# Three lag matrices loaded instead of made, the down weights turned last, the clip sigmoids earlier

## The chip, the cores and the metric

The kernel runs on one core of a Trainium2 chip. Its time is device microseconds (us) of one launch; lower is better. The engines of the core are named as in the profile: PE (TensorE) for matrix products, PEld for its weight loads, DVE (VectorE), ACT (ScalarE), POOL (GpSimd), and SP (SyncE), which here issues nearly all DMAs. Each engine works through its own list of instructions in the order of the code, and semaphores tie the lists together.

## The reference

The layer adds two gated branches to x (32 sequences of 128 tokens, 256 channels). The first is a two-sided decaying sum over time of the context (keys and values are both `ctx`), times the sigmoid of the normalised x. The second is a gated feed-forward network on fake-quantised activations and weights.

```python
def birwkv(r, k, v, w, u):                 # w, u: one value a channel
    ew, ek = exp(w), exp(k)
    Af, Bf = scan(ek, v, ew)               # A_t = sum_{i<t} e^{(t-1-i)w + k_i} v_i;  B_t without v
    Ab, Bb = the same from the other end
    cur = exp(u + k)
    return sigmoid(r) * (Af + Ab + cur * v) / (Bf + Bb + cur)

def quant(x, clip):                        # one scale for the whole tensor
    s = sigmoid(clip) * max|x| / 127
    return clip(round(x / s), -128, 127) * s

x = x + tanh(g_xattn) * birwkv(layernorm(x), ctx, ctx, w, u)
z = quant(layernorm(x), clip_x)
h = quant(silu(z @ Wg.T) * (z @ Wu.T), clip_down)
x = x + tanh(g_ffn) * (h @ Wd.T)           # each W quantised with a scale for each row
```

## The kernel before

**Stages.** The whole of x stays in SBUF. (1) x and ctx are loaded; ctx is turned round in time by PE (`reverse`), and exp(k) and exp(k)·v are kept in `hidden`. (2) The sum over time is, for each channel, a product with a 128x128 matrix of decays ("lag matrix"). The 256 channels are worked in 32 chunks of 8 channels; `accumulate(j)` is chunk j: eight matrices, each times 64 or 128 columns. (3) Second layernorm, `turn_z` (transposes on PE) and the largest value. (4) Quantisation, gate and up products, the largest value again. (5) Quantisation, down products, the last addition and the stores.

**Lag matrices.** The 8 matrices of a chunk are 512 KB. They lie in a ring of six slots of `hidden`. For 26 chunks SP loads them by one DMA each from a small table in HBM, `lag_dram`, whose rows are read with an overlapping pattern (`load_lags`, L265). For the six chunks of `MADE` (10, 14, 18, 22, 26, 30) they are computed instead: ACT takes eight exponentials (`make_lags`, L591, L598), POOL multiplies the flipped identity by exp(u)-1 (`own_weights`, L375, L382, two halves) and adds it (`add_own`, L387, L392, two halves). A slot comes free for chunk j when chunk j-6 has been used (`ab_done`). PE waits for the DMA (`ring_in`) or for POOL (`made`).

**A chunk's way.** After `accumulate(j)` DVE computes the denominator into `den`, which lies in h_space (`denominator`, L735); for each pair m of chunks ACT takes Ln and Exp of it (`reciprocal`, L505 and L508); DVE multiplies (`mix`, L747), and POOL adds the pair to x (`residual`, L399). DVE's list takes denominators and mixes by turns: den(2m+2), mix(2m), den(2m+3), mix(2m+1). The last pair goes by halves (L516, L519, L407, and `residual_own` at L757 on DVE). A chunk's bank in PSUM, one of six, comes free when the chunk six before has been mixed (`mix_done`).

**Other work between the chunks.** The three weight matrices are loaded, and for each DVE finds the scales of its rows (`weight_scales`, L686 to L688), ACT quantises (L542) and casts it (L550), PE turns it (`turn_weights`, L969, behind chunks 14, 23 and 30) and ACT keeps it (L559). For the third, the down weights, DVE also scales two 128x128 identities (`down_diagonals`, L775). These stand in DVE's list behind pair 9. From pair 10 on DVE takes six layernorm statistics a pair of the half of x that is already final (`early_stats`, L704). The sigmoids of the two clip values are an Exp on ACT (`exp_clips`, L564, L566, at pair 12) and four small instructions on DVE (`sigmoid_clips`, L769, L770, at pair 13).

**Behind the chunks.** `late_stats` on DVE, four tiny powers and products on POOL (`rstd2`, L367 to L373), the normalisation on ACT (L527) and POOL (L433), `turn_z` on PE (L981) and `keep_z` on ACT (L534). Between groups 3 and 6 PE runs five products whose result isn't used (`idle_wide`, L1004).

Of the kernel before, what the change touches and what calls it, by code (L numbers as in the profile page):

```python
# [40 lines left out]
def gated_rwkv_ffn(nc, x, ctx_kv, g_xattn, g_ffn, w, u, clip_x, clip_down, w_gate, w_up, w_down, out):  # L41
# [19 lines left out]
    LAGS = 2 * T - 1  # L61
    SLOTS = 6

    MADE = 10, 14, 18, 22, 26, 30
    BANKS = 6
    HALF = CK * SEQS

# [3 lines left out]
    with ExitStack() as stack:  # L71
# [39 lines left out]
        def loads_to(n):  # L111

            return len([i for i in range(n % SLOTS, n + 1, SLOTS) if i - GROUPS not in MADE])

        def lag_tile(j):
            return ring[(GROUPS + j) % SLOTS].rearrange("p (g t) -> p g t", t=T)
# [133 lines left out]
        def _(sp):  # L250
# [14 lines left out]
            def load_lags(j):  # L265

                before = GROUPS + j - SLOTS
                if before < GROUPS:
                    sp.wait_ge(s["ctx_back"], before + 1)
                else:  # L270
                    sp.wait_ge(s["ab_done"], before - GROUPS + 1)
                src = bass.AP(lag_dram, j * CK * LAGS, [[1, P], [LAGS, CK], [1, T]])
                sp.dma_start(lag_tile(j), src).then_inc(ring_in[(GROUPS + j) % SLOTS], 16)  # L273
# [36 lines left out]
            for j in range(CHUNKS):  # L310
                if j not in MADE:
                    load_lags(j)
# [20 lines left out]
        def _(pool):  # L333
# [41 lines left out]
            def own_weights(i):  # L375

                j = MADE[i]
                pool.wait_ge(s["u_all_done"], 2)
# [8 lines left out]
            def add_own(i):  # L387
                for h in range(2):
                    pool.wait_ge(s["made_exp"], 2 * i + h + 1)
                    pool.wait_ge(s["own_done"], 2 * i + h + 1)  # L390
                    part = lag_tile(MADE[i])[:, h * CK // 2:(h + 1) * CK // 2, :]
                    nc.gpsimd.tensor_tensor(part, part, own_parts[h].rearrange("p (g t) -> p g t", t=T),  # L392
                                            ALU.add).then_inc(s["made"], 1)
# [25 lines left out]
            for m in range(PAIRS - 1):  # L419
                residual(m)  # L420
                j = 2 * (m + 1) + 6
                if j in MADE:
                    add_own(MADE.index(j))
                    if j != MADE[-1]:
# [44 lines left out]
        def _(act):  # L469
# [31 lines left out]
            def reciprocal(m):  # L501

                act.wait_ge(s["den_done"], 2 * m + 2)
                wait(act, s["rden_done"], m)
                nc.scalar.activation(lnd, den[:, m % 2, :], ACT.Ln).then_inc(s["ln_done"], 1)  # L505
                act.wait_ge(s["ln_done"], m + 1)
                wait(act, s["mix_done"], 2 * m - 2)
                nc.scalar.activation(rden[:, m % 2, :], lnd, ACT.Exp, scale=-1.0).then_inc(s["rden_done"], 1)  # L508
# [28 lines left out]
            def quantise_weights(m):  # L537

                act.wait_ge(s["w_rec"], m + 1)
                cols, parts, inverse = (C, KA, w_inv[:, m, :]) if m < 2 else (KA * P, CH, down_inv)  # L540
                for i in range(parts):
                    last = nc.scalar.activation(w_int[:, i * cols:(i + 1) * cols], w_nat[m][:, i * cols:(i + 1) * cols],  # L542
                                                ACT.Copy, scale=inverse[:, i:i + 1])
                last.then_inc(s["w_quant"], 1)

            def cast_weights(m):

                act.wait_ge(s["w_quant"], m + 1)
                wait(act, s["w_turned"], m)
                nc.scalar.activation(w_intb[:, :], w_int[:, :], ACT.Copy).then_inc(s["w_cast"], 1)  # L550

            def keep_weights(m):

                act.wait_ge(s["w_turned"], m + 1)
                banks = ps[:, TURN:TURN + 2, 0:KA * P // 2].bitcast(BF16)
                dst = (wgT[:, :, :], wuT[:, :, :], wdT[:, :, :].rearrange("p k (h n) -> p h k n", n=P))[m]
                if m == 2:
                    banks = banks.rearrange("p h (k n) -> p h k n", n=P)
                nc.scalar.activation(dst, banks, ACT.Copy).then_inc(s["w_stored"], 1)  # L559

            def exp_clips():

                act.wait_ge(s["clx_in"], 16)
                nc.scalar.activation(S["sgx"], S["clx"], ACT.Exp, scale=-1.0).then_inc(s["clips_done"], 1)  # L564
                act.wait_ge(s["cld_in"], 16)
                nc.scalar.activation(S["sgd"], S["cld"], ACT.Exp, scale=-1.0).then_inc(s["clips_done"], 1)  # L566
# [24 lines left out]
            def make_lags(i):  # L591

                j = MADE[i]
                act.wait_ge(s["lag_abs_done"], 1)
                act.wait_ge(s["ab_done"], j - SLOTS + 1)
                for c in range(CK):
                    n = j * CK + c
                    last = nc.scalar.activation(lag_tile(j)[:, c, :], lag_abs, ACT.Exp, scale=w_all[:, n:n + 1])  # L598
                    if c % (CK // 2) == CK // 2 - 1:
                        last.then_inc(s["made_exp"], 1)  # L600

            for m in range(PAIRS - 1):
                reciprocal(m)
                if 2 * m + 6 in MADE:
                    make_lags(MADE.index(2 * m + 6))
                if m in (3, 7, 11):
                    quantise_weights((3, 7, 11).index(m))
                if m in (9, 13):
                    keep_weights((9, 13).index(m))
                if m in (5, 9, 13):  # L610
                    cast_weights((5, 9, 13).index(m))
                if m == 12:
                    exp_clips()
            for j in (CHUNKS - 2, CHUNKS - 1):
                reciprocal_half(j)
# [50 lines left out]
        def _(dve):  # L666
# [60 lines left out]
            def denominator(j):  # L727

                dve.wait_ge(s["ab_done"], j + 1)
                if j == 0:  # L730
                    dve.wait_ge(s["ez_done"], GROUPS)
                m, i = j // 2, j % 2
                if i == 0:
                    wait(dve, s["ln_done"], m - 1)
                nc.vector.scalar_tensor_tensor(den[:, m % 2, i * HALF:(i + 1) * HALF].rearrange("p (c b) -> p c b", b=SEQS),  # L735
                                               ez[:, :, j * CK:(j + 1) * CK].rearrange("p b c -> p c b"), 1.0, half_bank(j, 0),
                                               ALU.add, ALU.mult).then_inc(s["den_done"], 1)

            def mix(j):
                m, i = j // 2, j % 2  # L740
                if m < PAIRS - 1:
                    dve.wait_ge(s["rden_done"], m + 1)
                else:
                    dve.wait_ge(s["rden_half"], i + 1)
                if i == 0:
                    wait(dve, s["x1_done"], m - 1)
                nc.vector.scalar_tensor_tensor(mixed[:, m % 2, i * CK:(i + 1) * CK, :], half_bank(j, 1), S["tanh_x"],  # L747
                                               rden[:, m % 2, i * HALF:(i + 1) * HALF].rearrange("p (c b) -> p c b", b=SEQS),
                                               ALU.mult, ALU.mult).then_inc(s["mix_done"], 1)
# [45 lines left out]
            for m in range(PAIRS - 2):  # L795
                denominator(2 * m + 2)
                mix(2 * m)
                denominator(2 * m + 3)
                mix(2 * m + 1)
                if m == 2:  # L800
                    weight_scales(0)
                if m == 6:
                    weight_scales(1)
                if m == 9:
                    weight_scales(2)
                    dve.wait_ge(s["ident_set"], 2)
                    down_diagonals()
                if m == 13:
                    sigmoid_clips()
                if m > 9:  # L810
                    early_stats(done, 6)
                    done += 6
# [120 lines left out]
        def _(pe):  # L933
# [27 lines left out]
            def turn_weights(m):  # L961

                pe.wait_ge(s["w_cast"], m + 1)
                wait(pe, s["w_stored"], m)
                for h in range(CH):
                    bank = ps[:, TURN + h, 0:KA * P // 2].bitcast(BF16)
                    for k in range(KA):
                        at_ = k * C + h * P if m < 2 else (h * KA + k) * P
                        last = nc.tensor.transpose(bank[:, k * P:(k + 1) * P], w_intb[:, at_:at_ + P], ident_b[:, :])  # L969
                last.then_inc(s["w_turned"], 1)  # L970
# [25 lines left out]
                    idle_products(5)  # L996
            for j in range(CHUNKS):
                accumulate(j)
                if j in (14, 23, 30):
                    turn_weights((14, 23, 30).index(j))  # L1000
            def idle_wide(n):

                for i in range(n):
# [110 lines left out]
```

## Time and profile before

| | us |
|---|---|
| three runs, median (lowest to highest) | 217.41 (217.23 to 217.84) |
| the profiled execution, its own time | 216.45 |
| its span, first to last instruction | 214.6 |
| busy: PE, DVE, ACT, POOL | 171.4, 171.0, 156.1, 137.6 |
| moved by DMA | 29.30 MB |

Time outside the span is 1.85 us. The profiled execution lies 0.96 us below the median of the runs. The chain of work that ended last names PE for 35% of the span, DVE for 22%, ACT for 15% and DMA for 9%. The chunks run from about 37 to 100 us, the second layernorm from there to 126 us.

### The profile page before, as it was taken

How to read it: one execution, taken by the hardware profiler on the slowest of the kernel's cores; microseconds unless marked ns; L12 is line 12 of the kernel's file. 1: busy time of each engine (PE TensorE's matmuls, PEld its weight loads, DVE VectorE, ACT ScalarE, POOL GpSimd, SP SyncE). 2: the span in 40 equal slices, each digit the busy share in tenths (PEclk: the TensorE clock that was granted, in tenths of full speed). 3: DMA queues.
4: the chain of work that ended last, by engine and by line, in shares of the span. 5: the costliest groups of instructions: out<-in, count | busy, mean ns of one | idle time of the engine just before them, and what ended most of it. 6: DMA issues, size and time to landing. Idle time of an engine off the chain costs nothing.

```text
span 214.6 us, 3377 instructions
## 1 busy us (share of the span) xinstructions
PE 171.4 (80%) x1121; PEld 124.1 (58%) x1126; DVE 171.0 (80%) x346; ACT 156.1 (73%) x237; POOL 137.6 (64%) x158
## 2 busy tenths in 40 slices
PE   4499977979899999974079888599799925989950
PEld 4456527979899999974057543234243403766620
DVE  0769495546657779999789779997999998999992
ACT  3459698555887896997789978588789834899300
POOL 3364223458599889995788808759886750039991
PEclk9969997999999999999556999999999995799995
DMA  3999999999999997300000000000000000004558
GB/s 92 346 358 348 349 322 292 286 283 292 290 305 292 227 260 220 101 2 2 0 0 0 0 5 0 0 0 0 3 0 0 0 0 0 3 0 147 175 195 268
DMA packets 43327, 29.30 MB, mean 137 GB/s; under 512 B 2224, under 2 KB 43056, under 8 KB 43312
## 3 DMA queue, kind: packets, MB, share of 16 engines
q1 hardware_dynamic: 43168, 28.84, 47.0%
q10 hardware_dynamic: 144, 0.26, 0.3%
q8 instruction: 9, 0.15, 0.3%
q14 instruction: 6, 0.05, 0.1%
HBM read 24.65 MB, written 4.46 MB: 136 GB/s over the span
## 4 chain that ended last, share of the span: by engine, by line
PE 35%; DVE 22%; ACT 15%; DMA 9%; issue 7%; SPq 6%; POOL 3%; DVEq 1%; ACTq 0%
PE ps L1050 9%; PE ps L1083 9%; PE ps L941 7%; PE ps L957 7%; DMA hidden<-lag_w 6%; DVE hidden L847 4%; DMA hidden<-in_ctx 3%; ACT hidden L527 3%; SPq L273 2%; DVE h_space L904 2%; DVE hidden L865 2%; PE ps L988 2%; DVE h_peaks L876 2%; ACT hidden L598 2%; ACT silu_out L648 2%
## 5 line engine op out<-in xcount | busy, mean ns | idle before, releaser
L957 PE MATMUL ps<-hidden 128*128 128x128 f32 (+1 forms) x512 | 60.6, 280 | 5.7 <-DVE hidden L678 2.5
L957 PEld LDWEIGHTS ps<-hidden 128*128 128x128 f32 x512 | 59.5, 196 | 7.2 <-DMA hidden<-lag_w 5.7
L876 DVE TENSOR_REDUCE h_peaks<-hidden (+2 forms) x24 | 25.9, 1122 | 2.0 <-POOL hidden L452 1.3
L1083 PE MATMUL ps<-wdT,z_t 128*128 128x256 bf16 (+1 forms) x192 | 25.2, 286 | 2.7 <-ACT z_t L662 2.7
L735 DVE SCALAR_TENSOR_TENSOR h_space<-z_t,ps 128x256 f32<-128x256 f32 x32 | 19.0, 597 | 10.2 <-PE ps L957 10.0
L399 POOL TENSOR_TENSOR x_all<-x_all,silu_out 128x512 f32<-128x512 f32 x15 | 22.8, 1533 | 6.1 <-DVE silu_out L747 6.0
L662 ACT ACTIVATE z_t<-h_space 128x1024 bf16<-128x1024 int8 (+3 forms) x12 | 20.1, 1754 | 6.8 <-DVE h_space L904 6.8
L1083 PEld LDWEIGHTS ps<-wdT,z_t 128*128 128x128 bf16 (+1 forms) x192 | 17.1, 101 | 10.8 <-issue 4.8
L648 ACT ACTIVATE silu_out<-ps,mix_scale 128x1024 f32<-128x1024 f32 (+1 forms) x18 | 18.4, 1020 | 5.8 <-PE ps L1050 3.4
L465 POOL TENSOR_TENSOR x_all<-x_all,z_t 128x512 f32<-128x512 f32 x6 | 10.7, 1803 | 15.5 <-DVE z_t L922 15.5
L981 PE MATMUL ps<-ident,hidden 128*128 128x128 f32 x64 | 11.8, 345 | 10.4 <-POOL hidden L433 9.0
L497 ACT ACTIVATE z_t<-x_all,mr,nr 128x256 f32<-128x256 f32 x32 | 16.4, 589 | 3.7 <-POOL mr L361 3.7
L941 PE MATMUL ps<-hidden,flip 128*128 128x512 f32 x32 | 16.1, 645 | 3.2 <-DMA hidden<-in_ctx 3.2
L747 DVE SCALAR_TENSOR_TENSOR silu_out<-ps,small,silu_out 128x256 f32<-128x256 f32 x32 | 15.2, 477 | 4.3 <-ACT silu_out L508 2.6
L452 POOL TENSOR_TENSOR hidden<-silu_out,up_out 128x1024 f32<-128x1024 f32 x6 | 14.4, 2408 | 5.6 <-ACT up_out L652 5.4
L696 DVE BATCH_NORM_STATS2 bn<-x_all 128x6 f32<-128x256 f32 x32 | 11.2, 413 | 8.0 <-DMA x_all<-in_x 7.8
L452 POOL TENSOR_TENSOR hidden<-h_space 128x1024 f32<-128x1024 f32 x6 | 14.4, 2400 | 4.8 <-ACT h_space L652 4.8
L981 PEld LDWEIGHTS ps<-ident,hidden 128*128 128x128 f32 x64 | 9.7, 181 | 13.1 <-ACT hidden L527 11.8
L505 ACT ACTIVATE up_out<-h_space 128x512 f32<-128x512 f32 x15 | 9.3, 623 | 9.3 <-DVE h_space L735 9.3
L904 DVE TENSOR_SCALAR h_space<-hidden,small 128x1024 int8<-128x1024 f32 (+3 forms) x12 | 15.2, 1332 | 0.1
L356 POOL TENSOR_TENSOR ve<-mv,consts 128x4 f32<-128x4 f32 x8 | 1.6, 200 | 20.4 <-DVE mv L700 20.4
L598 ACT ACTIVATE hidden<-down_row,xq 128x128 f32<-128x128 f32 x48 | 14.6, 388 | 0.0
(109 smaller groups left out, 357.3 us busy)
## 6 DMA issues: line engine op xcount, KB each, us to landing
hidden<-lag_w SPq DMA_DIRECT2D x26, 512.0 KB, 7.3
x_all<-in_x SPq DMA_DIRECT2D x8, 512.0 KB, 8.8
hidden<-in_ctx SPq DMA_DIRECT2D x8, 512.0 KB, 9.1
out<-x_all SPq DMA_DIRECT2D x16, 256.0 KB, 2.4
xq<-in_L_ffn_w_down SPq DMA_DIRECT2D x1, 704.0 KB, 6.1
xq<-in_L_ffn_w_gate SPq DMA_DIRECT2D x1, 640.0 KB, 7.0
h_space<-in_L_ffn_w_up SPq DMA_DIRECT2D x1, 640.0 KB, 5.9
lag_w<-up_out ACTq DMA_DIRECT2D x1, 255.0 KB, 7.4
```

The lines of the kernel that those rows point to most:

```text
L399: nc.gpsimd.tensor_tensor(xs, xs, mixed[:, m % 2, :, :].rearrange("p c b -> p b c"), ALU.add).then_inc(s["x1_done"], 1)
L452: nc.gpsimd.tensor_tensor(hidden[:, b * HB + k * BT:b * HB + (k + 1) * BT], silu_even[n % 2], up_even[n % 2], ALU.mult).then_inc(s["h_even ...
L648: nc.scalar.activation(silu_out[:, 1, 0:cols] if k % 2 else silu_even[even % 2], banks[0], ACT.Silu, scale=mix_scale[:, 0, k:k + 1]).then_ ...
L662: nc.scalar.activation(hq[:, b % 2, cols], h8[:, b % 2, cols], ACT.Copy).then_inc(s["hq_done"], 1)
L735: nc.vector.scalar_tensor_tensor(den[:, m % 2, i * HALF:(i + 1) * HALF].rearrange("p (c b) -> p c b", b=SEQS), ez[:, :, j * CK:(j + 1) * C ...
L876: nc.vector.tensor_reduce(h_peaks[:, bass.ds(KA * b + k, 1)], hidden[:, bass.ds(b * HB + k * BT, cols)], AX.X, ALU.max, apply_absolute_val ...
L904: nc.vector.tensor_scalar(h8[:, b % 2, k * BT:last], hidden[:, b * HB + k * BT:b * HB + last], S["inv_h"], None, ALU.mult).then_inc(s["h8_ ...
L941: last = nc.tensor.matmul(turned(g)[:, half], flip[:, :], ring[g % SLOTS][:, half], start=True, stop=True)
L957: last = nc.tensor.matmul(ps[:, j % BANKS, c * 2 * SEQS:end * 2 * SEQS], lag_tile(j)[:, c, :], ekp[:, (j * CK + c) * 2 * SEQS:(j * CK + en ...
L981: last = nc.tensor.transpose(ps[:, z_bank(g) + h, i * T:(i + 1) * T], z_all[:, n * C + h * P:n * C + (h + 1) * P], ident[:, :])
L1050: last = nc.tensor.matmul(dst, wT[:, h, k * P:k * P + rows_], whole_x(b)[:, j, h, :], start=(h == 0), stop=(h == CH - 1))
L1083: last = nc.tensor.matmul(ps[:, 4 * sl + i, j * C:(j + 1) * C], lhs, rhs, start=(k == 0 and j == 0), stop=(k == KA - 1), skip_group_check= ...
```

## The change

Chunks 22, 26 and 30 leave `MADE`: SP loads their matrices like the others', ACT no longer takes their exponentials, and POOL no longer builds and adds for them. The turning of the down weights moves from between chunks 30 and 31 to behind chunk 31. The Exp of the clips moves from pair 12 to pair 9 on ACT, the rest of their sigmoids from pair 13 to pair 10 on DVE.

```diff
-    MADE = 10, 14, 18, 22, 26, 30
+    MADE = 10, 14, 18
...
-                if m == 12:
+                if m == 9:
                     exp_clips()
...
-                if m == 13:
+                if m == 10:
                     sigmoid_clips()
...
             for j in range(CHUNKS):
                 accumulate(j)
-                if j in (14, 23, 30):
-                    turn_weights((14, 23, 30).index(j))
+                if j in (14, 23):
+                    turn_weights((14, 23).index(j))
+            turn_weights(2)
+
             def idle_wide(n):
```

POOL's list, from the additions for chunk 22 (L392) to the first half residual (L407). `up_out` and `own` are the two halves of the products of `own_weights`; L399 is a residual. Before:

```order
L392 TENSOR_TENSOR hidden<-hidden,up_out 128x512
L392 TENSOR_TENSOR hidden<-hidden,own 128x512
L382 TENSOR_TENSOR up_out<-flip,xq 128x512
L382 TENSOR_TENSOR own<-flip,xq 128x512
L399 TENSOR_TENSOR x_all<-x_all,silu_out 128x32x16 x2
L392 TENSOR_TENSOR hidden<-hidden,up_out 128x512
L392 TENSOR_TENSOR hidden<-hidden,own 128x512
```

After, all that is left between the additions for chunk 18 and the end of the stage:

```order
L392 TENSOR_TENSOR hidden<-hidden,up_out 128x512
L392 TENSOR_TENSOR hidden<-hidden,own 128x512
L399 TENSOR_TENSOR x_all<-x_all,silu_out 128x32x16 x9
L407 TENSOR_TENSOR x_all<-x_all,silu_out 128x32x8
L407 TENSOR_TENSOR x_all<-x_all,silu_out 128x24x8
```

So twelve instructions of L382 and L392 are gone there, and nine residuals follow each other directly.

PE's list, from chunk 30 to the first transpose of the next stage (L981), with the semaphores waited for, as one piece of the difference:

```order
-L957 MATMUL ps<-hidden 128x128 [waits mix_done,made]
+L957 MATMUL ps<-hidden 128x128 [waits mix_done,ring_in2]
+L957 MATMUL ps<-hidden 128x128 x6
+L957 MATMUL ps<-hidden 128x64
+L957 MATMUL ps<-hidden 128x128 [waits mix_done,ring_in3]
 L957 MATMUL ps<-hidden 128x128 x6
 L957 MATMUL ps<-hidden 128x64
 L969 MATMUL ps<-ident_b,w_intb 128x128 [waits w_stored,w_cast]
 L969 MATMUL ps<-ident_b,w_intb 128x128 x11
-L957 MATMUL ps<-hidden 128x128 [waits mix_done,ring_in3]
```

Chunk 30 now waits for a DMA, not for POOL, and the wait for ACT's cast (`w_cast`) stands behind chunk 31.

## Rows read from the trace of the kernel before

**Rows 1.** The page, 40 slices of 5.4 us: PE's granted clock in tenths.
```profile
PEclk9969997999999999999556999999999995799995
```

**Rows 2.** Windows of 10 us: busy us of each engine, clock, DMA share, GB/s.
```profile
70.00:80.00 10.00, 9.73 (x88) 9.59 (x87) 7.06 (x15) 9.22 (x20) 8.62 (x8) 1.00 0.96 242
80.00:90.00 10.00, 10.00 (x98) 10.00 (x97) 9.86 (x22) 7.83 (x17) 9.71 (x9) 1.00 0.65 187
```

**Rows 3.** Timeline of DVE at pair 9: start, us, instruction, [idle before, releaser].
```profile
77.95 0.48 DVE L747 SCALAR_TENSOR_TENSOR silu_out<-ps,small,silu_out 128x256 f32<-128x256 f32 x1 [1.16 <-ACT silu_out L508]
...
79.26 1.74 DVE L686 TENSOR_REDUCE small<-xq 128x2 f32<-128x1536 f32 x1
81.04 0.83 DVE L687 TENSOR_SCALAR small<-small 128x2 f32<-128x2 f32 x1
...
81.98 2.65 DVE L775 TENSOR_SCALAR down_diag<-ident,small 128x128 f32<-128x128 f32 x2
```

**Rows 4.** Timeline of POOL over the same time.
```profile
80.30 3.03 POOL L399 TENSOR_TENSOR x_all<-x_all,silu_out 128x512 f32<-128x512 f32 x2
83.28 1.28 POOL L392 TENSOR_TENSOR hidden<-hidden,up_out 128x512 f32<-128x512 f32 x1
```

**Rows 5.** Timeline of DVE: the same scaling for the two other weight matrices.
```profile
53.75 0.17 DVE L687 TENSOR_SCALAR w_scale<-w_scale 128x6 f32<-128x6 f32 x1
...
69.60 0.86 DVE L687 TENSOR_SCALAR w_scale<-w_scale 128x6 f32<-128x6 f32 x1
```

**Rows 6.** Groups of DVE by form: count, busy us, mean ns of one.
```profile
L852 DVE TENSOR_SCALAR hidden<-z_t,small 128x512 int8<-128x512 f32 x2 | 0.9, 484 | 0.2 <-DVE small L839 0.2
```

**Rows 7.** Timeline of PE, chunks 22 to 31 (16 records a chunk) and the turns.
```profile
78.21 3.79 PE L957 MATMUL ps<-hidden 128*128 128x128 f32 x32 [0.27 <-POOL hidden L392]
...
82.50 10.88 PE L957 MATMUL ps<-hidden 128*128 128x128 f32 x96
94.27 2.00 PE L957 MATMUL ps<-hidden 128*128 128x128 f32 x16 [0.89 <-POOL hidden L392]
96.93 0.84 PE L969 MATMUL ps<-ident_b,w_intb 128*128 128x128 bf16 x12 [0.66 <-ACT w_intb L550]
97.61 1.95 PE L957 MATMUL ps<-hidden 128*128 128x128 f32 x16
```

**Rows 8.** Timeline of DVE over the last pairs.
```profile
94.60 0.60 DVE L735 SCALAR_TENSOR_TENSOR h_space<-z_t,ps 128x256 f32<-128x256 f32 x1
...
95.50 0.15 DVE L769 TENSOR_SCALAR small<-small 128x1 f32<-128x1 f32 x1
...
96.27 1.26 DVE L704 BATCH_NORM_STATS2 bn<-x_all 128x6 f32<-128x128 f32 x6
97.44 0.59 DVE L735 SCALAR_TENSOR_TENSOR h_space<-z_t,ps 128x256 f32<-128x256 f32 x1
...
99.60 0.58 DVE L735 SCALAR_TENSOR_TENSOR h_space<-z_t,ps 128x256 f32<-128x256 f32 x1
...
101.63 0.27 DVE L757 TENSOR_TENSOR x_all<-x_all,silu_out 128x64 f32<-128x64 f32 x1
```

**Rows 9.** Timeline of ACT: the eight exponentials for chunk 22.
```profile
74.31 2.43 ACT L598 ACTIVATE hidden<-down_row,xq 128x128 f32<-128x128 f32 x8
```

**Rows 10.** SP: the last eight loads (timeline); issue to landing from 64 us on.
```profile
69.55 17.08 SPq L273 DMA_DIRECT2D hidden<-lag_w  x8
...
DMA to landing us min/median/max: 3.9/4.5/7.7
```

**Rows 11.** Timeline of PE in the stage behind the chunks.
```profile
112.76 1.94 PE L981 MATMUL ps<-ident,hidden 128*128 128x128 f32 x8 [0.79 <-POOL hidden L433]
...
116.81 1.03 PE L1004 MATMUL ps<-wgT,ident_b 128*128 128x512 bf16 x4
...
120.07 1.06 PE L981 MATMUL ps<-ident,hidden 128*128 128x128 f32 x8 [0.20 <-issue]
```

**Rows 12.** Window of 2 us, as rows 2; clock before the DMA's two figures.
```profile
116.00:118.00 2.00, 1.95 (x12) 1.28 (x12) 1.75 (x10) 2.00 (x4) 1.76 (x6) 0.90 0.00 0
```

## The prediction, made before the changed kernel was timed

> **What bounds the kernel now.** I read windows of 10 us first, then the timeline of each engine around what the diff touches, and last the slices for the clock. In the window from 80 to 90 us PE and DVE are both full, 10.00 and 9.86 us of 10 [rows 2]. With two engines at the limit, the question is whose lag is carried to the last chunk. PE takes 10.88 / 6 = 1.81 us a chunk when it waits for nothing [rows 7], so 3.62 us a pair. DVE's work of a pair is shorter: a denominator and its mix take 95.50 - 94.60 = 0.90 us, the six statistics 97.44 - 96.27 = 1.17, so a pair 2 x 0.90 + 1.17 = 2.97 [rows 8]. DVE would therefore wait for PE, but it doesn't, since at pair 9 it fell behind: it is busy with the down weights' scales from 79.26 to 84.63, while chunks 22 and 23 were long done, at 78.21 + 3.79 = 82.00 [rows 3, 7]. It catches up 0.6 us a pair and meets PE again only at chunk 31, whose denominator at 99.60 stands right behind the product's end, 97.61 + 1.95 = 99.56 [rows 7, 8]. PE for its part lost time to POOL before chunks 22 and 30 (0.27 and 0.89 us) and to the cast and the turn before chunk 31 [rows 7].
>
> **DVE's long block is a wait in disguise.** The scaling L687 of two elements takes 0.83 us at pair 9, and 0.86 us at the second matrix, but 0.17 us at the first [rows 3, 5]. At pair 9 it starts at 81.04 inside POOL's first residual (80.30 + 1.51 = 81.81) and ends at 81.87. The first diagonal starts at 81.98 inside the second residual, which ends at 83.33; the second follows, beside POOL's addition from 83.28 to 84.56, and ends at 84.63 [rows 3, 4]. Each of the three ends 0.06 to 0.1 us after a POOL instruction: they stand still until POOL's is over. The sigmoids' scaling of one element took 0.15 us with POOL busy, so not every scaling is held [rows 8].
>
> **Part 1, the three chunks loaded.**
> ACT loses three times eight exponentials, 2.43 us each time [rows 9]. At pair 8 this lets ACT start the Ln of pair 9 1.2 us sooner (it needs a denominator that is there), so DVE no longer stands 1.16 us before mix 18 [rows 3]. But denominator 21 behind it has to wait for chunk 21, which ends at 77.94, just before PE's wait [rows 7]; so the block of the down weights starts only 0.4 us sooner, at 78.9.
> POOL loses for each of the chunks two additions of 1.28 us [rows 4] and two products. What follows at pair 9 changes: residual 9 needs mix 19, and runs from about 79.0 to 80.55; residual 10 needs mix 21, which comes after the block. The reduce takes 1.74 us to 80.6 (I assume it isn't held: it took that beside POOL before), then L687 finds POOL idle. I take its 0.17 us [rows 5], and 0.25 us for a diagonal of 128 elements, between 0.17 for six and 0.48 for 512 [rows 5, 6]. The block then ends at about 78.9 + 1.78 + 0.2 + 0.2 + 0.5 = 81.6 instead of 84.63: 3.0 us sooner. From there the next pair needs chunk 23, done at 81.6 too.
> PE starts chunk 22 at 77.9 instead of 78.21, turns the up weights, whose cast is ready, and runs chunks 24 to 31 without a break: 82.50 - 0.3 + 8 x 1.81 = 96.7 instead of 99.56. DVE now waits for PE by chunk 29: that ends at 82.2 + 6 x 1.81 = 93.1, so denominator 29 comes at 93.1 instead of 94.60, 1.5 us sooner.
> SP and the DMAs: three more loads, 1.57 MB, in a stretch where the DMA engines moved 242 and 187 GB/s [rows 2]. The ring lets load j go when chunk j-6 is used. A load took 4.5 us to land [rows 10]; at 0.96 busy the engines moved 242 GB/s, so 0.524 MB costs between 1.81 us (if 290 GB/s are had) and 2.1 us (by 242 / 0.96 = 252). No row shows eleven in a stretch here; I take 1.8, as PE and loads kept step before. Chunk 21's was issued at 69.55 (the first of the last eight) [rows 10] and lands at about 74.0; ten more at 1.81 put chunk 31's at 92.1, at 2.1 us at 95.0; PE wants it at 94.9. So the loads hide, at the bad end just. Nothing else is queued behind them on SP until the stores.
> One thing goes the other way. At 69.60 the second matrix's L687 stood beside a product of POOL, which is gone; residual 6 takes its place and lasts 1.51 us [rows 4, 5], so L687 may end up to 0.65 us later. DVE's 1.16 us of idle time at mix 18 [rows 3] takes that in.
>
> **Part 2, the sigmoids.** They move from pair 13, 95.50 to 96.27 (0.77 us) [rows 8], to pair 10. There they sit in DVE's catching up, before it waits for PE, and cost nothing; in the tail they were all on the path: 0.77 us gained. Had the block not shrunk, DVE would be bound in both places and the move would be worth 0. ACT's Exp of the clips at pair 9 takes 0.2 us where ACT has time.
>
> **Part 3, the turn.** Chunk 31 no longer stands behind the cast (0.66 us) and the turn (0.67 us, 96.93 to 97.61) [rows 7]. This is in the 96.7 above. Left where it was, the turn would put chunk 31's end at 97.4 while DVE reaches that denominator at about 97.2: worth 0.2 us. In its new place ACT keeps the turned weights only after the last pair's Exp; the turn is done by 97.6, so nobody waits.
>
> **The sum.** Denominator 29 comes 1.5 us sooner, and from it to `residual_own` at 101.63 [rows 8] the tail is shorter by 0.77 (sigmoids) and about 0.1 (small waits for ACT and PE): 2.4 us. `residual_own` at 99.2 starts the statistics, and all behind is a chain through POOL, ACT and PE that moves as one. For the profiled execution: 216.45 - 2.4 = 214.05. It lay 0.96 below the median of the runs; for the median I predict 217.41 - 2.4 = **215.0 us**, by itself between 214.4 and 215.7, the spread of 0.6 of the runs included.
>
> By the Trainium skill (SBUF — State Buffer, Who interferes with whom) a `tensor_scalar` in a two-port mode and a GpSimd instruction lock each other out wholly for the length of the first, and whoever issues first wins. By that rule the hold is gone once POOL has nothing at that moment, and the kernel comes to the 215.0 above; if the block were simply 5.4 us long, to some 216.4. The trace speaks for the rule: 0.83 against 0.17 us for the same instruction [rows 3, 5].
>
> **Rivals.**
> *The hold stays* (0.13). Residual 9 starts when mix 19 ends and lasts 1.51 us, the reduce 1.74 us: L687 finds POOL idle by only 0.1 us. One residual under a diagonal holds the block 1.3 us, as before. DVE then is bound to the end: 0.4 sooner, plus about 0.6, so 217.41 - 1.0 = 216.4.
> *The loads end last* (0.06). If a load costs 2.1 us the gain is 2.0; at 2.3 us chunk 31 ends about where it did before, so 217.3, and above that the kernel is slower. Against: the engines are at 0.65 from 80 us on [rows 2].
> *Slower by the clock* (0.05). PE's clock is at its lower level, 1.2 GHz, after the chunks (fives and a six) [rows 1], and is back at 2.4 GHz from about 116.4: 0.90 of a 2 us window [rows 12]. PE now falls idle 2.4 us sooner too, so I let the return move along. If it doesn't, a group with idle products costs at the lower level 1.94 + 5 x 2 x 0.26 = 4.5 us against a pitch of (120.07 - 112.76) / 3 = 2.44 [rows 11]: 2.1 us a group. From a bit more than one such group on the change loses; two give 217.41 - 2.4 + 4.2 = 219.2. For it: the return need not follow the work, and I can't tell from one trace what holds it. Against: before, it came while PE ran nothing but transposes, ahead of the first idle product at 116.81 [rows 11, 12], and the transposes move along.
> The Trainium skill (TensorE: Matmul & The Clock Gate, Part 4: PE-mode transpose) says transposes don't count as busy for the clock gate. By it the clock returns only behind the idle products, which is this rival. The trace disagrees: it came back at 116.4 before the first of them.
> *More* (0.06). An earlier return of the clock gives up to 0.9 us (the first transposes, 1.94 against 1.06) [rows 11]: about 214.3.
>
> **The numbers.** Forecast 0.70; hold 0.13, loads 0.06, clock 0.05, more 0.06. The range 214.1 to 216.6 takes in forecast, hold and more, less their tails: about 0.85. A measurement can tell 0.3%, 0.65 us. Faster than that: 0.70 + 0.11 + 0.06 = 0.87; within it 0.06 (weak hold, half of the loads); slower 0.07.
>
> **What would show it.** Right: L775 twice under 0.6 us together, first denominator of pair 10 at 81.7; no wait of PE for a DMA after chunk 22; chunks 24 to 31 in 14.5 us; `residual_own` at 99.2; the clock back by 116.4. Wrong: L775 over 1 us; PE waiting for `ring_in`; a second group of idle products at 1.2 GHz.

## The result: 213.8 us in the first measurement, 2.4 to 2.6 us gained over many executions

| | before | after |
|---|---|---|
| first measurement, median (lowest to highest) | 217.32 us (216.35 to 217.84), 4 | 213.82 us (213.55 to 214.46), 4 |
| ratio | | 0.985, interval 0.981 to 0.989 |
| the profiled execution | 216.45 us | 214.46 us |
| its span | 214.6 us | 212.7 us |
| busy PE, DVE, ACT, POOL | 171.4, 171.0, 156.1, 137.6 | 170.4, 168.3, 149.3, 124.5 |
| moved by DMA | 29.30 MB | 30.88 MB |
| all executions of the study, mean (lowest to highest) | 217.34 us (214.84 to 220.26), 93 | 214.73 us (213.03 to 216.40), 18 |

I had predicted 215.0 us, between 214.1 and 216.6. The change is faster, as forecast, but the measured 213.82 lies below the range. The last line of the table came out of the experiments and turns out to be what matters: the gain is 2.6 us with a standard error of 0.23 (from 0.97 / sqrt(93) and 0.91 / sqrt(18)), not 3.5. Twelve of the 93 executions before count as slow, being over 1.5% above the fastest of their measurement; the ratios in this document leave such executions out, and without them the mean before is 217.14 us and the gain 2.4 us.

The trace of the changed kernel shows the steps nearly to the letter. DVE at pair 9, timeline (compare [rows 3]):

```profile
79.52 1.75 DVE L686 TENSOR_REDUCE small<-xq 128x2 f32<-128x1536 f32 x1
81.30 0.17 DVE L687 TENSOR_SCALAR small<-small 128x2 f32<-128x2 f32 x1
81.50 0.17 DVE L688 RECIPROCAL small<-small 128x2 f32<-128x2 f32 x1
81.59 0.59 DVE L775 TENSOR_SCALAR down_diag<-ident,small 128x128 f32<-128x128 f32 x2
82.21 0.60 DVE L735 SCALAR_TENSOR_TENSOR h_space<-z_t,ps 128x256 f32<-128x256 f32 x1
```

POOL at that time, after (compare [rows 4]):

```profile
79.69 1.54 POOL L399 TENSOR_TENSOR x_all<-x_all,silu_out 128x512 f32<-128x512 f32 x1 [2.02 <-DVE silu_out L747]
84.17 1.54 POOL L399 TENSOR_TENSOR x_all<-x_all,silu_out 128x512 f32<-128x512 f32 x1 [2.94 <-DVE silu_out L747]
```

The residual ends at 79.69 + 1.54 = 81.23 and L687 starts at 81.30, 0.07 us later. L687 takes 0.17 instead of 0.83 us, the diagonals 0.59 together instead of 2.65, and the block from L686 to the last diagonal 2.66 us instead of 5.37. PE, after (compare [rows 7]):

```profile
64.75 3.74 PE L957 MATMUL ps<-hidden 128*128 128x128 f32 x32
69.43 12.72 PE L957 MATMUL ps<-hidden 128*128 128x128 f32 x112 [0.95 <-DMA hidden<-lag_w]
81.99 0.83 PE L969 MATMUL ps<-ident_b,w_intb 128*128 128x128 bf16 x12
82.66 14.46 PE L957 MATMUL ps<-hidden 128*128 128x128 f32 x128
96.95 0.83 PE L969 MATMUL ps<-ident_b,w_intb 128*128 128x128 bf16 x12
```

Chunks 24 to 31 are one stretch of 14.46 us (128 records), with no wait for POOL, a load or ACT's cast. The one wait, 0.95 us at 69.43, is for chunk 17's load, ahead of everything that the change touches. DVE over the last pairs, after (compare [rows 8]):

```profile
93.58 0.60 DVE L735 SCALAR_TENSOR_TENSOR h_space<-z_t,ps 128x256 f32<-128x256 f32 x1 [0.52 <-PE ps L957]
94.10 0.47 DVE L747 SCALAR_TENSOR_TENSOR silu_out<-ps,small,silu_out 128x256 f32<-128x256 f32 x1
94.49 1.25 DVE L704 BATCH_NORM_STATS2 bn<-x_all 128x6 f32<-128x128 f32 x6
...
97.57 0.58 DVE L735 SCALAR_TENSOR_TENSOR h_space<-z_t,ps 128x256 f32<-128x256 f32 x1
...
99.60 0.27 DVE L757 TENSOR_TENSOR x_all<-x_all,silu_out 128x64 f32<-128x64 f32 x1
```

DVE waits for PE at denominator 29, and the statistics follow mix 27 without the sigmoids between. `residual_own` comes at 99.60 instead of 101.63, 2.03 us sooner, and that is the 1.99 us by which the profiled executions differ. The clock after, on the page (compare [rows 1]):

```profile
PEclk9969999999999999999557999999999995899995
```

The clock comes back to 2.4 GHz at 114.6 us, from a granted clock of 0.86 in the window from 114 to 116, against 116.4 before: 1.8 us sooner, with the work.

So the two traces say 2.0 us, my sum 2.4, the first medians 3.5. The experiments had to settle two questions: is the mechanism the one I gave, and where do the other 1.5 us come from.

### The profile page after: what moved, and what is told of

The parts are those of the page before. It is cut to its first block, busy times and chain, and to the rows that moved or that the text cites. A ratio compares the mean times of both kernels' runs of the same rounds, so it can differ in the third digit from the quotient of the medians.

```text
span 212.7 us, 3337 instructions
## 1 busy us (share of the span) xinstructions
PE 170.4 (80%) x1126; PEld 123.2 (58%) x1126; DVE 168.3 (79%) x346; ACT 149.3 (70%) x213; POOL 124.5 (59%) x146
## 2 busy tenths in 40 slices
DMA packets 46448, 30.88 MB, mean 145 GB/s; under 512 B 2272, under 2 KB 46176, under 8 KB 46432
## 4 chain that ended last, share of the span: by engine, by line
PE 45%; DVE 21%; DMA 10%; ACT 10%; issue 5%; SPq 3%; POOL 3%; DVEq 1%; ACTq 0%
PE ps L957 19%; PE ps L1052 9%; PE ps L1085 9%; DMA hidden<-lag_w 7%; PE ps L941 5%; DVE hidden L847 4%; DMA hidden<-in_ctx 4%; ACT hidden L527 3%; PE ps L988 2%; DVE h_space L904 2%; DVE hidden L865 2%; DVE h_peaks L876 2%; ACT silu_out L648 2%; DVE bn L704 2%; ACT z_t L534 2%
## 5 line engine op out<-in xcount | busy, mean ns | idle before, releaser
L957 PE MATMUL ps<-hidden 128*128 128x128 f32 (+1 forms) x512 | 58.5, 276 | 6.1 <-DMA hidden<-lag_w 3.7
L957 PEld LDWEIGHTS ps<-hidden 128*128 128x128 f32 x512 | 57.8, 192 | 7.4 <-DMA hidden<-lag_w 7.3
L399 POOL TENSOR_TENSOR x_all<-x_all,silu_out 128x512 f32<-128x512 f32 x15 | 23.1, 1541 | 19.2 <-DVE silu_out L747 19.2
L735 DVE SCALAR_TENSOR_TENSOR h_space<-z_t,ps 128x256 f32<-128x256 f32 x32 | 19.0, 598 | 10.4 <-PE ps L957 10.1
L981 PE MATMUL ps<-ident,hidden 128*128 128x128 f32 x64 | 11.8, 346 | 10.2 <-POOL hidden L433 8.7
L696 DVE BATCH_NORM_STATS2 bn<-x_all 128x6 f32<-128x256 f32 x32 | 11.2, 414 | 8.6 <-DMA x_all<-in_x 8.3
L981 PEld LDWEIGHTS ps<-ident,hidden 128*128 128x128 f32 x64 | 9.8, 182 | 12.9 <-ACT hidden L527 11.6
L1052 PE MATMUL ps<-xq,wuT 128*128 128x512 bf16 (+1 forms) x48 | 11.5, 381 | 3.6 <-DVE hidden L865 3.5
L988 PEld LDWEIGHTS ps<-ident,flip 128*128 128x128 f32 x64 | 11.1, 261 | 5.3 <-POOL ident_b L345 2.8
```

Source lines behind the costliest of these rows:

```text
L399: nc.gpsimd.tensor_tensor(xs, xs, mixed[:, m % 2, :, :].rearrange("p c b -> p b c"), ALU.add).then_inc(s["x1_done"], 1)
L957: last = nc.tensor.matmul(ps[:, j % BANKS, c * 2 * SEQS:end * 2 * SEQS], lag_tile(j)[:, c, :], ekp[:, (j * CK + c) * 2 * SEQS:(j * CK + en ...
L981: last = nc.tensor.transpose(ps[:, z_bank(g) + h, i * T:(i + 1) * T], z_all[:, n * C + h * P:n * C + (h + 1) * P], ident[:, :])
L1052: last = nc.tensor.matmul(dst, wT[:, h, k * P:k * P + rows_], whole_x(b)[:, j, h, :], start=(h == 0), stop=(h == CH - 1))
```

## The experiments

Each had its expectation on record before it ran. Since the executions of one kernel turned out to spread over 3 to 5 us, I read small differences not from the medians but from distances inside a trace: from DVE's denominator 20 (start of its L735) to `residual_own`, which is the stretch that the change touches; from `residual_own` to the first gate product; and from there to the largest value of h (L834).

| kernel | median us (executions) | ratio to before, interval | den. 20 to residual_own | to first gate product | to the peak of h |
|---|---|---|---|---|---|
| before, first trace | 217.32 (4) | | 25.44 | 26.80 | 49.06 |
| r1_before | 217.19 (12) | 0.9986, 0.9955 to 1.0016 | 25.07 | 27.12 | 50.39 |
| after, first trace | 213.82 (4) | 0.9848, 0.9807 to 0.9889 | 22.77 | 26.83 | 49.06 |
| r1_after | 214.80 (6) | 0.9861, 0.9803 to 0.9918 | 22.78 | 26.89 | 50.58 |
| r3_after | 215.27 (8) | 0.9910, 0.9871 to 0.9948 | 22.76 | 26.82 | 49.05 |
| r1_chunks | 216.17 (12) | 0.9934, 0.9890 to 0.9977 | 23.55 | 27.47 | 50.38 |
| r1_moves | 217.84 (12) | 1.0017, 0.9980 to 1.0053 | 25.61 | 26.80 | 50.65 |
| r2_hold | 216.83 (10) | 0.9980, 0.9936 to 1.0024 | 24.15 | 26.78 | 50.55 |
| r2_chunks_sig | 215.40 (10) | 0.9900, 0.9857 to 0.9944 | 23.02 | 26.84 | 49.05 |
| r2_gatefill | 213.86 (6) | 0.9854, 0.9803 to 0.9905 | 22.78 | 26.83 | 49.06 |
| r3_gatefill | 213.84 (6) | 0.9840, 0.9800 to 0.9879 | 22.78 | 26.81 | 49.06 |
| r3_before_gatefill | 216.29 (12) | 0.9983, 0.9947 to 1.0019 | 25.89 | 27.52 | 49.08 |
| r2_zfill | 214.82 (12) | 0.9882, 0.9848 to 0.9917 | 22.78 | 28.20 | 49.05 |
| r3_w19 | 214.29 (6) | 0.9854, 0.9817 to 0.9891 | 22.59 | 26.81 | 49.07 |

### Both kernels again

No edit.

> The kernel before, unchanged, run against itself for the scatter, and for a second trace of it. The first pair of traces moved by 2.0 us (216.45 to 214.46), the medians by 3.5 us (217.32 to 213.82). Theory A (the traces show all of the gain; the rest is scatter between few launches): this one is within 0.3% of the kernel before, 217.3 +/- 0.5, and its trace has the down weights' block again at about 5.4 us with three scalings held. Theory B (an ordinary launch of the kernel before is slower than the one traced, for a cause that the change removes): the second trace shows something longer than the first, 1 us or more, in front of residual_own, and says where.

> The changed kernel again. Theory A: 2.0 us faster than before, ratio 0.991, about 215.3. Theory B: 3.5 us faster, ratio 0.984, about 213.8. In the trace both expect L775 twice at 0.27 us, the first denominator of pair 10 at 82.2, and PE waiting for no load after chunk 22.

> The changed kernel a third time, to size the gain. Four executions gave a median of 213.8, six a median of 214.8. If the gain is what the traces show between denominator 20 and residual_own (25.3 to 22.8 us, 2.5 us), many executions give 2.5 +/- 0.5 us less than the kernel before, ratio 0.9885; if the first 3.5 us were the gain, 0.984 again.

The kernel before ranged from 214.93 to 218.91 us within one measurement of 29 executions. The second measurement of the change gave 0.986, the third 0.991: neither the 3.5 us again nor the 2.0 us, but 2.6 us over all. In the traces the touched stretch is always 22.76 to 22.78 us after. Before it is 25.07 and 25.44 us, and 25.89 in r3_before_gatefill, whose products stand behind this stretch: 2.3 to 3.1 us. That the first pair of traces differed by only 2.0 comes from outside this stretch: denominator 20 came at 76.83 instead of 76.19. In the after trace PE stood for two loads between 54 and 78 us, 0.52 us for chunk 11's and 0.95 us for chunk 17's, in the kernel before for chunk 11's alone, 0.65 us. In r3_after PE ran chunks 15 to 23 in one piece:

```profile
66.31 16.24 PE L957 MATMUL ps<-hidden 128*128 128x128 f32 x144
```

It had stood 1.47 us for chunk 11's load instead, and its denominator 20 came at 77.24, later still. Such waits ahead of the stretch differ from one execution to the next, in both kernels: 0.6 to 1.8 us between 54 and 78 us in the fourteen traces.

Theory B is half right: the ordinary launch does lose time that the first traces didn't show, but both kernels lose it, as the later experiments show.

### The parts alone

r1_chunks is the kernel before with this edit alone:

```diff
-    MADE = 10, 14, 18, 22, 26, 30
+    MADE = 10, 14, 18
```

r1_moves is the kernel before with the other edits of the change and `MADE` as it was. r2_chunks_sig is the changed kernel with the turn where it was:

```diff
-                if j in (14, 23):
-                    turn_weights((14, 23).index(j))
-            turn_weights(2)
+                if j in (14, 23, 30):
+                    turn_weights((14, 23, 30).index(j))
```

> Only the three chunks are loaded instead of made; the sigmoids stay at pair 13 and the turn before chunk 31. My steps: the hold of the down weights' block goes (3.0 us earlier), PE runs on; the tail keeps 0.77 us of sigmoids and the turn costs 0.2. So 1.0 us less gain than the full change: by theory A ratio 0.995 (-1.1 us), by theory B 0.989 (-2.4 us).

> Only the sigmoids (pair 10) and the turn (behind chunk 31) move; the chunks 22, 26 and 30 are still made. My steps: DVE is bound from pair 9 on, so moving the sigmoids gains nothing; the turn lets chunk 31 go 1.3 us sooner, but DVE comes to its denominator only at 99.55: at most 0.2 us gained, ratio 0.999 to 1.000. A rival, that the turn before chunk 31 was the bound, gives 0.5 to 1.3 us, ratio 0.994 to 0.998.

> The changed kernel with the turn of the down weights left between chunks 30 and 31. My step: chunk 31 ends 0.7 us later, DVE is nearly there: residual_own 0.2 us later than in the changed kernel, seen from denominator 20 (22.8 us there) 23.0 us. Rival: PE waits for the cast too, 0.7 us or more. In the time 0.2 us can't be told.

With the chunks alone the touched stretch is 23.55 us, 0.77 more than with all edits. That is what the two moves are worth together. With chunks and sigmoids it is 23.02: moving the sigmoids first gains 0.53, and the turn after them 0.24. DVE then waits 0.16 us for PE at the last denominator, where the changed kernel waits for nothing:

```profile
97.53 0.58 DVE L735 SCALAR_TENSOR_TENSOR h_space<-z_t,ps 128x256 f32<-128x256 f32 x1 [0.16 <-PE ps L957]
```

(I had expected 1.0 us for the two together. In r1_chunks the turn costs nothing: chunk 31 ends at 95.38 + 1.95 = 97.33, and DVE, late by the sigmoids, comes to its denominator only at 97.89, without a wait.)

The two moves without the chunks give nothing: 25.61 us, no better than the 25.07 to 25.89 before, and a ratio of 1.0017. Each of the small edits pays only behind the large one. What DVE wins by the sigmoids in r1_moves it loses again at once, waiting for ACT before mix 28:

```profile
98.25 0.88 DVE L747 SCALAR_TENSOR_TENSOR silu_out<-ps,small,silu_out 128x256 f32<-128x256 f32 x2 [0.79 <-ACT silu_out L508]
```

There ACT works without a break from 90.71, where it takes the eight exponentials for chunk 30 (2.43 us), up to the Exp of pair 14, which ends at 98.22. In the changed kernel these exponentials are gone. PE, too, still stands for POOL before chunk 30, for 1.67 us in this trace.

### POOL put back in DVE's way

```diff
                 residual(m)
+                if m == 9:
+                    pool.wait_ge(s["made"], 6)
+                    for n in range(3):
+                        if n == 2:
+                            pool.wait_ge(s["own_done"], 8)
+                        nc.gpsimd.tensor_tensor(own_parts[n % 2].rearrange("p (g t) -> p g t", t=T),
...
```

> The changed kernel, with three extra products of the L382 form (1.04 us each, result unused) on POOL directly behind residual 9, so that POOL is busy again while DVE is at the down weights' block, without any lag matrix being made. If the block was long because POOL holds DVE's scalings, L687 and the two L775 again take about 1 us each and end with POOL's products: the block ends about 2.2 us later than in the changed kernel (84.4 instead of 82.2) and, since DVE regains 0.6 us a pair, residual_own comes about 1.2 to 1.5 us later: time between the changed kernel and the kernel before, +1.3 us against the changed one. Rival (the gain came from PE and ACT being free of the made chunks): the block keeps its 2.6 us, L775 0.27 us, and the time is that of the changed kernel.

DVE, timeline of r2_hold (its lines stand 9 higher: L696 is the scaling, L784 the diagonals):

```profile
78.71 1.74 DVE L695 TENSOR_REDUCE small<-xq 128x2 f32<-128x1536 f32 x1
80.48 0.95 DVE L696 TENSOR_SCALAR small<-small 128x2 f32<-128x2 f32 x1
...
81.56 2.06 DVE L784 TENSOR_SCALAR down_diag<-ident,small 128x128 f32<-128x128 f32 x2
83.65 0.59 DVE L744 SCALAR_TENSOR_TENSOR h_space<-z_t,ps 128x256 f32<-128x256 f32 x1
```

POOL, same kernel:

```profile
78.87 1.55 POOL L399 TENSOR_TENSOR x_all<-x_all,silu_out 128x512 f32<-128x512 f32 x1 [0.83 <-DVE silu_out L756]
80.38 1.04 POOL L426 TENSOR_TENSOR up_out<-flip,xq 128x512 f32<-128x512 f32 x1
81.37 1.04 POOL L426 TENSOR_TENSOR own<-flip,xq 128x512 f32<-128x512 f32 x1
82.49 1.04 POOL L426 TENSOR_TENSOR up_out<-flip,xq 128x512 f32<-128x512 f32 x1
```

Three products that nobody reads, and the three scalings end at 81.43, 82.50 and 83.61, each with one of POOL's at 81.42, 82.41 and 83.53. The reduce at 78.71 runs its 1.74 us beside POOL's residual untouched. The block takes 4.90 us instead of 2.66, the first denominator of pair 10 comes 1.9 us later after denominator 20, and the stretch to `residual_own` grows by 1.37 (24.15), as expected. Over ten executions the mean is 216.69 us, 2.0 above the changed kernel's 214.73, with a standard error of 0.4 (1.8 without the highest of the ten). The hold is shown: only these three products differ between the two kernels, and the chunks are loaded in both. 1.37 of the 2.3 to 3.1 us, about half, is its absence at the least, as the three products put back a block of 4.90 us and not of 5.37. The Trainium skill (SBUF — State Buffer, Who interferes with whom) gives the rule: `tensor_scalar` can contend with GpSimd, `tensor_reduce` on this chip never; both halves agree with these rows.

### The clock in the gap of the first gate and up block

The time from the first gate product to the peak of h is 49.05 to 49.08 us or 50.38 to 50.65 us, nothing between, and both occur in both kernels. Windows of r1_before and of the kernel before (busy us of each engine, then PE's granted clock, DMA share, GB/s), the same stretch:

```profile
138.00:141.00 3.00, 3.00 (x10) 1.03 (x8) 2.97 (x4) 1.58 (x2) 0.28 (x1) 0.59 0.00 0
```

```profile
138.00:141.00 3.00, 3.00 (x16) 1.12 (x14) 3.00 (x3) 2.21 (x3) 0.80 (x1) 1.00 0.00 0
```

The first is r1_before. PE had stood idle 2.2 us ahead of it, in both and in the seven other traces without the products below, waiting for DVE's product L865. In r1_before the clock then fell to 1.2 GHz for a while (a mean of 0.59 over these 3 us) and ten products ran where sixteen did in the other.

The same edit, eight products in this gap, makes r2_gatefill and r3_gatefill out of the changed kernel, and r3_before_gatefill out of the kernel before:

```diff
+                            if b == 0 and k == 3:
+                                pe.wait_ge(s["silu_done"], 5)
+                                for i in range(8):
+                                    nc.tensor.matmul(ps[:, 0, :], ident_b[:, :], wgT[:, 0, 0:512], start=True, stop=True)
                             pe.wait_ge(s["h_odd"], ODD * (b + 1) + k // 2)
```

> The changed kernel, with eight products whose result is unused on PE in the gap of the first block of gate and up products (about 2.6 us idle before the fourth piece's up product). Theory A (the clock): in four of six traces so far the clock fell to 1.2 GHz for 3.4 us right behind this gap, and the stage from the first gate product to the last peak took 50.4 to 50.7 us, against 49.06 us in the two traces where it did not. With the gap filled the clock stays and the stage takes about 49.1 us each time: median 0.5 to 1.2 us below the changed kernel's 214.8, with less spread. Rival (the stage's length has another cause, or the products delay it): no change or slower by up to 1 us.

> The changed kernel with the eight products in the gap of the first gate and up block, again. Its first trace had no fall of the clock near the gap anyway, so it told nothing. Clock theory: the trace keeps 2.4 GHz from 125 to 170 us and the stage takes 49.1 us; the median is 0.8 us below the changed kernel's of this call. Rival: a trace with the clock fallen in spite of the products, and no difference.

> The kernel before with the same eight products. Clock theory: the same 0.8 us as there, so about 216.7, and against the changed kernel with the products it shows the change itself with one source of scatter less: 2.5 us. Rival (the change altered how often the clock falls there): 3.0 us or more between these two.

PE in r3_gatefill, the eight products in the gap and half a microsecond idle behind them:

```profile
132.91 1.89 PE L1039 MATMUL ps<-wgT,ident_b 128*128 128x512 bf16 x8
135.29 1.04 PE L1056 MATMUL ps<-xq,wuT 128*128 128x512 bf16 x4 [0.50 <-DVE hidden L865]
```

Without the products the clock fell in this place in five of nine traces (of both kernels and the variants), with them in none of five; chance alone would put all five falls among the nine once in 16 times. The changed kernel's executions with the products have a mean of 213.82 us (12) against 214.73 (18) without, 0.9 us less with a standard error of 0.29. For the kernel before the gain isn't shown: over all executions it is 0.7 us (216.60, 12, against 217.34), but against those of its own measurement the ratio is 0.9983, from 0.9947 to 1.0019. The difference between the two kernels with the products is 2.8 us, with a standard error of 0.3 (0.92 / sqrt(12) and 0.66 / sqrt(12)), as without them: nothing shows that the change alters how often the clock falls here. So this is a source of the scatter, common to both kernels, and no part of the gain. It also makes the filled kernel the fastest that I ran: 213.86 and 213.84 us in two measurements, ratios 0.985 and 0.984.

### The clock held through the transposes

```diff
             turn_weights(2)
...
+            pe.wait_ge(s["mix_done"], 29)
+            idle_wide(32, 4)
```

On top of the eight products; the second argument is the bank in PSUM.

> As the one before, and 32 more such products on PE behind the turn of the down weights, into the time of 8 us in which PE is idle before the transposes of z. Theory A (the clock): the clock stays at 2.4 GHz there, each of the first transposes takes 1.06 instead of 1.94 us, keep_z of group 0 starts 0.9 us sooner, and the stage from residual_own to the first gate product (26.8 us) takes 25.9 to 26.5 us: 0.3 to 0.9 us faster than the filled kernel. Rival (the stage is paced by the chain of DVE, POOL and ACT alone): 26.8 us again.

It went the other way: 28.20 us for a stretch of 26.8. PE of r2_zfill, timeline:

```profile
110.23 1.06 PE L981 MATMUL ps<-ident,hidden 128*128 128x128 f32 x8 [1.67 <-POOL hidden L433]
112.53 1.94 PE L981 MATMUL ps<-ident,hidden 128*128 128x128 f32 x8 [1.24 <-issue]
114.68 1.91 PE L1006 MATMUL ps<-wgT,ident_b 128*128 128x512 bf16 x4 [0.22 <-issue]
116.39 1.91 PE L981 MATMUL ps<-ident,hidden 128*128 128x128 f32 x8
```

The first three groups of transposes did run at 2.4 GHz, 1.06 us each. Between them PE was idle for 1.2 to 1.7 us, the clock fell before the fourth group, and it returned only behind 118 us. A group with its idle products then ran at 1.2 GHz, which is my slower rival: 1.94 us of transposes and over 1.9 of products, more than the pitch of 2.4.

The other thirteen traces show this place without the 32 products. In eleven of them the stretch is 26.8 to 27.1 us, in r1_chunks and r3_before_gatefill it is 27.47 and 27.52. In these two the clock stayed at 1.2 GHz through all of the first four groups and into the idle products. PE of r1_chunks, timeline:

```profile
113.36 1.94 PE L981 MATMUL ps<-ident,hidden 128*128 128x128 f32 x8 [0.36 <-issue]
115.52 1.91 PE L1004 MATMUL ps<-wgT,ident_b 128*128 128x512 bf16 x4 [0.22 <-issue]
117.23 1.19 PE L981 MATMUL ps<-ident,hidden 128*128 128x128 f32 x8
```

In r1_before, r1_after and r2_hold the third group ran at 2.4 GHz and the fourth at 1.2 GHz again, wholly or in part. So the trace of before, where the clock came back just ahead of the idle products, is one of several courses that one kernel can take here.

### The down weights loaded later

```diff
-                if j == 16:
+                if j == 19:
                     load_weights(2)
```

On top of the eight products.

> The changed kernel with the eight products, and the down weights loaded behind chunk 19's matrices instead of behind chunk 16's. In every trace of the changed kernel PE waited for chunk 17's load, which stands behind the 0.8 MB of the weights and landed at 68.0 to 69.4 us. With the weights behind it, it lands at about 66; PE is the bound from there to residual_own, so all of the wait, 0.3 to 1.4 us, is gained: median 0.7 us below the filled kernel. Rival (the loads are the bound: the same bytes end at the same time, and PE waits at chunks 20 to 23 instead): no difference.

No difference (214.29 against 213.84 us, the intervals overlap). Its premise was wrong: PE did not stand before chunk 17 in r1_after, r3_after and r3_gatefill, whose load landed in time; only the first after trace has that wait. Chunk 17's load did land earlier, 6.4 us after its issue instead of 6.8 to 8.5. But there was nothing to gain. What all fourteen traces do have is a wait of PE for chunk 11's load, which SP issues behind the up weights': 0.5 to 1.8 us, 1.81 in this trace. The edit doesn't touch it, and I tried nothing there.

## Why the prediction was right and where it failed

**The hold (3.0 us on the block): right.** The block shrank by 2.71 us. The first denominator of pair 10 came 2.46 us sooner, and 3.10 us sooner counted from denominator 20, which was 0.64 us late in this execution; I had 3.0. The diagonals took 0.27 and 0.28 us; I had taken 0.25. The rival "the hold stays" hung on 0.1 us between residual 9 and L687; the nine traces without chunks 22 to 30 in `MADE` and without products put back show 0.05 to 0.08, and L687 takes 0.17 us in all nine. That this is so steady isn't luck: the residual and the reduce both start right behind mix 19.

**PE and the loads: right.** Eleven loads in a row kept ahead of PE; chunks 24 to 31 took 14.46 us, I had 8 x 1.81 = 14.5. From issue to landing a load took 7.3 us in the median now, not 4.5 [rows 10]; they still came in time. The page's slices from 74 to 90 us have 297, 293 and 290 GB/s, so the 290 GB/s on which the good end of my estimate hung were had.

**Sigmoids 0.77 and turn 0.2: right one by one, not as a sum.** The turn measures 0.24 with the sigmoids moved. The sigmoids measure 0.53 with the turn where it was; with the turn moved they must be worth 0.77, by r1_chunks, where the turn costs nothing, but I didn't run that kernel. Together they are worth 0.77 and not 0.97. That the moves are worth nothing alone is right, though not only for my reason: DVE wasn't bound to the end there, it waited 0.79 us for ACT.

**The sum of 2.4 us: right.** The touched stretch is 2.3 to 3.1 us shorter, the mean of many executions 2.4 to 2.6 lower, and 217.34 - 2.4 = 214.9 is within 0.25 us of the mean of the changed kernel.

**The range: wrong, by one term.** The step that failed is "between 214.4 and 215.7, the spread of 0.6 of the runs included". I took three executions that lay within 0.6 us for the scatter of the kernel. Its standard deviation is 0.97 us and its extremes 5.4 us apart. The median of four executions has by that a standard error of about 1.25 x 0.9 / 2 = 0.6 us, so an 80% range for it needs 0.7 us on either side before any doubt on the sum. The median of the first four executions of the changed kernel, 213.82, lay 0.9 us below the mean of its eighteen. The mean of those four is 213.92 us and that of the other fourteen 214.96: 1.0 us apart, two standard errors (0.91 x sqrt(1/4 + 1/14) = 0.5). So the 3.5 us of the first measurement were for the greater part the luck of four executions, as far as these numbers tell; that something else favoured that measurement isn't excluded. My low end was 0.9 below the forecast, all of it meant for a better clock, with nothing left for this.

**The rival "slower by the clock": it happens, at a third of its price.** A return of the clock one group later occurred in two traces, r1_chunks and r3_before_gatefill. I had 2.1 us for it; the stretch grew by 0.7. As one of them loads the three chunks and the other makes them, it looks like scatter and not like an effect of the change; two traces don't prove it. That "the return moves along" held in the first trace after, but one trace of before couldn't show it.

**The cause of the scatter** I had in view, but as a rival with 0.05 and in the wrong place. Three sources are visible in traces of unchanged work: the clock behind the gap in the first gate and up block, 1.3 to 1.6 us or nothing; the return of the clock among the transposes (26.8 to 27.5 us for that stretch); and what lies before denominator 20 (21.0 to 22.3 us from denominator 8), with PE's waits for loads, 0.6 to 1.8 us between 54 and 78 us, in it. They are enough to span 3 us. How much each holds of the total I haven't measured: with the first filled, the standard deviation was 0.66 instead of 0.91 us on the changed kernel, but 0.92 and 0.97 on the kernel before.

What stays open: what decides in a given execution whether the clock falls, and why three traces with the lists of before differ by 0.8 us in the touched stretch (PE's wait for POOL before chunk 22 is 0.27 us in the first and 0.73 in the longest, r3_before_gatefill, and r1_before has none).

## What to carry to other kernels

When a tiny DVE instruction takes a microsecond, look at what GpSimd does at that moment: taking work off POOL can free DVE, though DVE waits for none of its results. Price small edits together with the large one, since which engine ends last decides whether they are worth all or nothing. And before giving a range, ask how far one kernel's executions lie apart: three that agree say little when the clock can fall or not in a gap, and a distance inside the trace can tell a few tenths where the medians can't: 0.02 us apart in three traces of the changed kernel, though 0.8 in three of the kernel before.

## What the hardware showed that I had not expected

- Behind a gap of 2.2 us on PE the clock fell in some executions and not in others of the same program, at 1.3 to 1.6 us each time; with eight idle products in the gap it stayed in five traces of five.
- Making PE faster made the kernel slower: in r2_zfill three groups of transposes ran at 2.4 GHz, 1.06 us each, then the clock fell and the stretch took 28.20 instead of 26.8 us. That is one trace, and what made the clock fall isn't shown. With the transposes at 1.2 GHz the clock was back by the idle products or during them in most traces, and in r1_chunks and r3_before_gatefill only behind the first of them.
- DVE's scaling of 2, 6 or 128 elements was held by a POOL instruction already running, up to its end (0.83, 0.86 and 1.20 to 1.43 us instead of 0.17, 0.17 and 0.27). The scaling of one element (0.15 us for L769), the reciprocal (0.17 us for L697 in r2_hold), the statistics (six in 1.25 us) and the reduce were not: the reduce takes 1.74 or 1.75 us beside POOL's products as beside its residual.
